# Signals of half groups that wait for TensorE's finished products and a pause on ScalarE, in the two relation layers of a graph network kernel

## The reference

```
# layer 0
msg = relu((x[src] * weight[:, None]) @ W_msg + b_msg)
x   = layernorm(x + relu(segment_sum(msg, dst) @ W_out + b_out))
# layers 1 and 2, the relation layers; h starts as x
xt  = einsum('nd,rde->rne', h, w)            # 8 products for every node
agg = segment_sum(xt[kind, src], dst)
h   = relu(agg + h @ sl + b)                 # w1, sl1, b1, then w2, sl2, b2
# the end
out = layernorm(x + h)
```

## Time and profile before

| | us |
|---|---|
| median of 3 runs | 7146.97 |
| the profiled execution | 7199.0 |
| its span, first to last instruction | 7197.2 |
| code layer 0 and all before it, to the first gather from `rel_table` | 2594.2 |
| code layer 1, first to last gather | 2272.4 |
| from there to the first gather of code layer 2 | 44.0 |
| code layer 2, first to last gather | 2255.5 |
| from there to the end | 31.1 |
| busy: PE 2514.6, PEld 2050.0, DVE 2687.2, ACT 608.2, POOL 4549.9 | |

### The profile page before, as it was taken

One profiled execution on the slowest core, in us unless ns is written; L12 is line 12 of the kernel. 1 busy time (PEld: TensorE's weight loads), 2 busy tenths in 40 slices (PEclk: granted clock), 3 DMA queues, 4 the chain that ended last, 5 costly groups with the idle time before them and its releaser, 6 DMA issues.

```text
span 7197.2 us, 44937 instructions
## 1 busy us (share of the span) xinstructions
PE 2514.6 (35%) x11886; PEld 2050.0 (28%) x11886; DVE 2687.2 (37%) x5889; ACT 608.2 (8%) x1334; POOL 4549.9 (63%) x4832
## 2 busy tenths in 40 slices
PE   4333344333444333433333343333222222222223
PEld 4332233222333322322222233222222222222222
DVE  3777566666555532332222332232111111111112
ACT  2111111111111110000000000000000000000000
POOL 4666666666666646666666666665666666666665
PEclk9666666666666666666666666665556565555556
DMA  5122222222222212222222222221111111121111
GB/s 144 43 79 74 69 73 71 74 70 75 72 72 74 74 58 63 69 69 69 66 70 68 69 69 66 67 68 56 52 51 51 52 51 52 52 53 52 51 51 48
DMA packets 265650, 468.76 MB, mean 65 GB/s; under 512 B 102413, under 2 KB 155317, under 8 KB 265381
## 3 DMA queue, kind: packets, MB, share of 16 engines
q0 software_dynamic: 154016, 315.73, 16.9%
q1 hardware_dynamic: 110212, 149.64, 6.1%
q10 hardware_dynamic: 1152, 0.39, 0.0%
HBM read 343.36 MB, written 122.05 MB: 65 GB/s over the span
## 4 chain that ended last, share of the span: by engine, by line
another core or an unknown queue 48%; DVE 23%; issue 17%; PE 9%; DVEq 2%; ACT 1%; DMA 0%; POOL 0%; SPq 0%; ACTq 0%; POOLq 0%
PE bank L787 5%; DVE rows L763 5%; DVE onehot L745 4%; PE bank L1047 3%; DVE picked L1087 3%; DVE place L1099 2%; DVE tab L1108 1%; DVEq L771 1%; DVE agg L776 1%; DVE bank L1410 1%; DVE work L1411 1%; DVE bank L1408 1%; DVE y L1143 1%; DVE stats L1147 1%
## 5 line engine op out<-in xcount | busy, mean ns | idle before, releaser
L698 POOL DMA_INDIRECT rows<-rel_table,rel_index x3152 | 2973.6, 943 | 1664.4 <-issue 931.5
L787 PE MATMUL bank<-onehot,rows 128*128 128x128 f32 x9626 | 1772.3, 357 | 3320.3 <-issue 1405.4
L787 PEld LDWEIGHTS bank<-onehot,rows 128*128 128x128 f32 x9626 | 1659.1, 265 | 3512.7 <-issue 1537.6
L698 POOL DMA_INDIRECT rows<-msg_table,msg_index x1597 | 1508.8, 945 | 929.0 <-issue 464.7
L776 DVE TENSOR_TENSOR agg<-agg,bank 128x128 f32 x602 | 171.4, 285 | 3613.6 <-remote 3150.7
L745 DVE TENSOR_TENSOR onehot<-bank,place 128x1024 f32<-128x1024 f32 x602 | 728.4, 1210 | 10.6 <-ACT agg L964 3.8
L1047 PE MATMUL bank<-wr,feat 128*128 128x512 f32 x784 | 521.3, 801 | 395.4 <-ACT feat L979 322.0
L763 DVE SCALAR_TENSOR_TENSOR rows<-rows,weight,bank 128x128 f32<-128x128 f32 x1597 | 428.6, 341 | 0.1
L1099 DVE TENSOR_REDUCE place<-picked 128x128 f32<-128x1024 f32 x196 | 367.4, 1875 | 19.8 <-DVE picked L1087 0.5
L668 ACT ACTIVATE rows<-rows 128x512 f32<-128x512 f32 x416 | 260.8, 629 | 1250.7 <-DVE rows L763 705.8
L1047 PEld LDWEIGHTS bank<-wr,feat 128*128 128x128 f32 x784 | 194.2, 275 | 564.8 <-ACT feat L979 332.5
(11 more groups left out here) (123 smaller groups left out, 1285.0 us busy)
## 6 DMA issues: line engine op xcount, KB each, us to landing
rel_table<-tab SPq DMA_DIRECT2D x196, 512.0 KB
rows<-rel_table,rel_index POOLq DMA_INDIRECT x3152
rows<-msg_table,msg_index POOLq DMA_INDIRECT x1597
x_dram<-normed SPq DMA_DIRECT2D x98, 64.0 KB
xin<-x_dram SPq DMA_DIRECT2D x98, 64.0 KB
xin<-in_x_dram SPq DMA_DIRECT2D x97, 64.0 KB
out_dram<-normed SPq DMA_DIRECT2D x97, 64.0 KB
tab<-in_x_dram SPq DMA_DIRECT2D x24, 256.0 KB
```

The lines of the kernel that those rows point to most:

```text
L698: nc.gpsimd.indirect_dma_start(rows[:, u, t, :], None, table, bass.IndirectOffsetOnAxis(ap=table_index[:, g, t:t + 1], axis=0)).then_inc(e ...
L787: ins = nc.tensor.matmul(ps_edge[k][:, 0:P], tile, onehot[:, k, t, :], start=t == 0, stop=t == tiles - 1)
```

## The change

A scratch tile `breath`, a semaphore `s_breath` and a helper `act_pause` are new: ACT copies 512 columns of a weight tile into the scratch tile and waits for its own copy. In the code layers 1 and 2 (`SPACED`) `act_ready` now waits before each half group until TensorE has finished all the products given so far, then pauses, then waits for the rows and signals. For this, `pe_group` raises a new semaphore `half` at the end of a first half. `act_first` also waits for the end of the group that was signalled just before it. In code layer 1 the two table products, the own product and the sum of picked rows no longer follow one another freely: TensorE waits for `go` before each but the first, and ACT gives `go` (in `act_spacing`) after it has seen the end of the one before (`part`, `prod`) and has paused.

```diff
+    SPACED = (1, 2)
...
+        breath = work[:, 7 * GROUP - 512:7 * GROUP]
...
+        def act_pause():
+            pauses[0] += 1
+            nc.scalar.activation(breath, wr[0][:, 0:512], ACT.Copy).then_inc(s_breath, 1)
+            nc.scalar.wait_ge(s_breath, pauses[0])
+
+        def products_idle(layer, sems, st, h):
+            if st.late or layer not in SPACED:
+                return
+            if h:
+                nc.scalar.wait_ge(sems.half, st.n + 1)
+            else:
+                need(nc.scalar, sems.prod, st.n)
+            if layer:
+                act_pause()
+
         def act_ready(layer, sems, st):
...
             for h in range(2):
                 if layer == 0:
                     nc.scalar.wait_ge(sems.scaled, st.n * 2 + (h + 1))
+                    products_idle(layer, sems, st, h)
                     v = rows[:, st.u, h * HALF:min((h + 1) * HALF, tiles), :]
                     nc.scalar.activation(v, v, ACT.Relu).then_inc(sems.ready, 1)
                 else:
+                    products_idle(layer, sems, st, h)
                     nc.scalar.wait_ge(sems.rows[st.u][h], gathered(st, h))
                     nc.scalar.sem_inc(sems.ready, 1)
...
                     ins = nc.tensor.matmul(ps_edge[k][:, 0:P], tile,
                                            onehot[:, k, t, :], start=t == 0, stop=t == tiles - 1)
-            ins.then_inc(sems.prod, 1)
+                ins.then_inc(sems.prod if h else sems.half, 1)
...
                     nc.scalar.wait_ge(edge_main.added, min(groups, COUNT[layer]) + FIRST[layer])
+                    if layer in SPACED:
+                        nc.scalar.wait_ge(edge_main.prod,
+                                          min(groups + 1, COUNT[layer]) + FIRST[layer])
...
+        def act_spacing(layer, sems, stage):
+            st = stage(PRODUCTS[layer]) if layer < 2 else None
+            if st is not None:
+                nc.scalar.wait_ge(sems.part, st.n + 1)
+                act_pause()
+                nc.scalar.sem_inc(sems.go, 1)
+                nc.scalar.wait_ge(sems.prod, st.n + 1)
+                if batch_end(st) and not short_batch(st):
+                    act_pause()
+                    nc.scalar.sem_inc(sems.go, 1)
+                    nc.scalar.wait_ge(sems.own, st.n + 1)
+            st = stage(PRODUCTS[layer] + 2) if layer < 2 else None
+            if st is not None and batch_end(st):
+                act_pause()
+                nc.scalar.sem_inc(sems.go, 1)
...
+            if trim and layer in SPACED:
+                act_spacing(layer, sems, stage)
...
                 nc.tensor.wait_ge(sems.feat, st.n + 1)
+                spaced = trim and layer in SPACED
                 for h in range(2):
+                    if h and spaced:
+                        nc.tensor.wait_ge(sems.go, gone(st.n))
                     ins = nc.tensor.matmul(table_banks(layer, st, trim)[h][:, :],
                                            feat[:, st.u, :],
                                            wr[layer][:, h * H:(h + 1) * H], start=True, stop=True)
+                    if not h:
+                        ins.then_inc(sems.part, 1)
                 ins.then_inc(sems.prod, 1)
                 if batch_end(st) and not (trim and short_batch(st)):
+                    if spaced:
+                        nc.tensor.wait_ge(sems.go, gone(st.n) + 1)
                     pe_own(layer, sems, st, trim)
...
                 nc.tensor.wait_ge(sems.pick, PICKS * (st.n + 1))
+                if layer in SPACED:
+                    nc.tensor.wait_ge(sems.go, gone_join(st.n))
```

More of the change, by code:

```diff
@@ L290, in __init__ @@
                     self.joined = sem(f"{name}_joined")
+                    self.go = sem(f"{name}_go")
+                    self.part = sem(f"{name}_part")
                 if table:
@@ L297, in build @@
         s_cut = sem("s_cut")
+        s_breath = sem("s_breath")
         s_pool_turn = sem("s_pool_turn")
@@ L310, in __init__ @@
                 self.prod = sem(f"{name}_prod")
+                self.half = sem(f"{name}_half")
                 self.added = sem(f"{name}_added")
@@ L657, in act_index @@
                     "p g t -> p (g t)"), ACT.Copy).then_inc(sems.index, 1)
+        pauses = [0]
+        def act_pause():
[11 more added lines that the diff above has]
+                act_pause()
         def act_ready(layer, sems, st):
@@ L985, in act_first, with gone, gone_join @@
                                          ).then_inc(sems.sums, 1)
+        def gone(b):
+            return b + 1 + b // UNROLL + max(b - 1, 0) // UNROLL
+        def gone_join(b):
+            return min(b + 2, BLOCKS) + (b + 1) // UNROLL + b // UNROLL + 1
+        def act_spacing(layer, sems, stage):
[13 more added lines that the diff above has]
+                nc.scalar.sem_inc(sems.go, 1)
         def act_nodes(layer, stage, trim):
```

## The result

The change made the kernel slower: 7364.16 us (median of 4 runs, 7342.25 to 7384.45) against 7147.12 (4 runs), a ratio of 1.0305 with a 95% interval of 1.0273 to 1.0336. The forecast was 6680, and the range began at 6570 and ended at 7900; the time lies in the range, on the side of the rival that was given less chance.

What follows compares the result with a forecast made beforehand. The prediction took POOL's gathers, plus its waits for late TensorE signals, to bound the kernel: 7197.2 - 302 - 247 = 6648, plus 80 left standing, 6728, + 1.8 - 52 = 6678, rounded to 6680; range 6570 to 7900.

Steps and rivals of the forecast that it cites:

- left 80 standing: Both relation layers: an eighth of POOL's 624.5 us of waits kept, since the layer starts show spaced halves held.
- What bounds the kernel: Both relation layers: POOL's gathers set a floor of 1970 us; waits for late TensorE signals add 302 and 285.
- if holds go: Both relation layers: gaps between TensorE's runs free most late signals, 302 and 247 us less; chance 0.55.
- the layer's start: Relation layer starts: halves already spaced by some 3 us idle, yet later additions waited 20.91 and 43.30 us.
- Which group an addition belongs to: Code layer 2 timeline: the addition at 6057.31 was read as that of the group ending by 6034.7.
- Half group and pause: Relation layers: 0.2 wait, 0.87 pause, 2.07 products, 2.93 us a half; no cost in code layer 2 while POOL is behind.
- Code layer 1's chain of 20.7 us a block: Code layer 1: ScalarE's waits and pauses in turn take 20.7 us a block against POOL's 20.0, binding narrowly.
- lower end: Likeliest case's bound of 6560: below by 59 us for a free table chain and 80 for the residue.
- Start and turn: Code layer 1's start and the turn: 40 us added to 98 blocks of 20.7, giving 2069.
- The slower rival: Both relation layers: late signals stay and are waited for one by one, 893 us more, 8040; chance 0.33.
- The full clock: Relation layers: pauses keep TensorE at half clock, used in the sum; full clock would make it 59 us less.
- CHAIN: Follow-up theory, relation layers: TensorE's late signals in their chain of additions and one-hot matrices set the pace, 11.4 us a group.

Runs made afterwards that it cites:

- rests kernel: Kernel before with small memsets as breaks in POOL's gather issuing in both relation layers; 7177.04 against 7193.01 us, ratio 0.9981, late signals.
- change_c: The changed kernel itself measured again beside the kernel before, with prompt signals; 6095.08 against 6082.67 us, ratio 1.0023.

## Why the prediction was wrong

The forecast took 302 us off code layer 2 with its tail and 247 off code layer 1 with the turn, and left 80 standing. In the profiles these parts grew, by 61.8 and 103.6 us.

- **What bounds the kernel.** Right in the measure: 302 and 285 us above POOL's floor, spent in stops of POOL for late signals. Wrong in that it took the stops for an effect of TensorE's way of working. Their sum hardly moves with TensorE's records, columns or gaps, nor with rows.
- **The failed step is "if holds go", that most of them go with the gaps.** In its place the runs showed that spaced half groups are signalled late as well: 126 of 393 in the changed kernel's code layer 2, and runs of 64 columns at 11.45 us a group where 10.0 to 10.4 would have been due. The count that the step rests on, none of 31 short runs held and all of 37 longer ones, doesn't come out of the trace. With each group's last record set against its own addition, and an idle time of over 0.5 us taken as the start of a run, 27 of 74 waited-for signals behind runs below 4.5 us were late and 77 of 78 behind longer ones; with 1 us as the bound, 11 of 38 and 93 of 114. One of the short ones, 3.79 us long behind 5.10 us of idle time:

```profile
5255.53 3.79 PE L787 MATMUL bank<-onehot,rows 128*128 128x128 f32 x16 [5.10 <-ACTq L671]
...
5285.03 0.29 DVE L776 TENSOR_TENSOR agg<-agg,bank 128x128 f32 x1 [29.61 <-remote]
...
5295.03 0.29 DVE L776 TENSOR_TENSOR agg<-agg,bank 128x128 f32 x1 [8.13 <-remote]
```

It ends at 5259.3 and is added at 5295.0. What is left of the link may run the other way: several groups come free at once behind a late signal, and TensorE runs them in one go. That is argued. The rows that could tell cause from effect were the layer's start, where gaps were there first, and they said that gaps don't help. They were given 0.33.
- **Which group an addition belongs to.** VectorE adds a group only behind the one-hot matrix of the next (`edge_step`). The addition at 6057.31 in the earlier trace rows is therefore that of the group that ended at 6022.1, not of the one that ended at 6034.7: the signal was 35 us late, where the prediction's reading gives 23.
- **Half group and pause.** Right: 2.86 us from half to half where 2.93 was forecast (0.87 and 2.07; the 0.2 that stands before them was not added), 0.79 for a pause with its handovers where it was 0.87. In code layer 2 they cost nothing with prompt signals, as worked out.
- **Code layer 1's chain of 20.7 us a block** was not to be seen with prompt signals: 1966.2 us for 98 blocks, 20.06 each, the POOL floor. The added-up chain was too long, as the prediction's lower end allowed for.
- **Start and turn.** Left at 40 us. With late signals the turn became 89.5, since what is left over at the layer's end now runs with pauses and at a granted clock of 0.61 instead of 0.85, where POOL has nothing to do: 45 to 51 us, and 14 to 24 in the tail. This term was missed: turn and tail are over a third of the loss.
- **The slower rival** had the mechanism (late signals are waited for one by one, rows above) and not the size: 1.65 us a group and 5.8 a block were forecast, 0.24 a group in code layer 2 (47.5 / 197) and 0.59 a block in code layer 1 (58.1 / 98) were measured. It assumed that a stop of 6.2 us must follow every two groups; there were 71 waits in 197 groups, 4.8 us each, and in the rests kernel POOL's idle time goes by the number of gathers.
- **The full clock.** The granted clock sank from 0.65 and 0.58 to 0.55 and 0.50. The Trainium skill ("TensorE: Matmul & The Clock Gate", "Why this matters for your kernels") says that idle gaps between bursts bring TensorE back to half rate, and the trace agrees. With prompt signals the two layers took 1966 us each at 0.58 and 0.50 (change_c), no more than in any other kernel; what the lower clock cost shows in the turn only.

That gaps don't free the signals, that in code layer 1 the waits cost and the pauses don't, that POOL's idle time is the same in breaks and stops, and that ScalarE is held too when it raises semaphores, is shown by runs. That a queue behind POOL is what delays the signals is argued, and CHAIN and a shared path of updates stand beside it.

## What to carry to other kernels

When two things in a steady cycle go together, look for a place where the supposed cause stands without the effect (the start of a stage, a turn) before building on it; here a few rows of a start should have outweighed 68 of the cycle. Before counting such pairs, find out from the code which instruction waits for which; here the addition in view belonged to the group before. Stops of an engine are best tested by giving it breaks of its own: if the sum stays, the engine has that time to spare, and something else sets the pace. Waits that are free while another engine is behind come to light in each turn and tail, so those are summed apart.

## What the runs showed of the hardware

The same program takes 6082 to 6094 us or 7147 to 7193 us. In the second, TensorE's signals are late while POOL issues gathers: in code layer 2 of the kernel before half of the groups are added over 11 us after their last record and a quarter over 31 us, at most 77.5 (19.7 in the changed kernel), against 0.5 at most with prompt signals (change_c). In the turn, where POOL issues none, they come at once. ScalarE is held for 0.7 to 1.4 us between increments that it otherwise makes every 0.07 us. A gather costs 1.43 us in the sum in code layer 2 instead of 1.25, whatever its rows, and 1.47 to 1.49 in code layer 0, which takes 2571 to 2594 instead of 2118 to 2125 us. The gathers' own packets are as quick as before. The late traces also hold fewer of the semaphore events: of the changed kernel's code layer 2 some 7,100 against 30,900 in the prompt trace. TensorE's records are complete in both (11886). So the path that records events and the one that carries signals may be the same one, or be slow for the same reason; no run here tells, and none shows whether the late kind exists in an execution that isn't recorded. No version that beats both kernels came out: the breaks gained 0.2% with late signals, near what can be measured, and would cost what they last with prompt ones.
